# A graph layer on one core: x low by adding loads, counts relieved in pairs, zero products, and the order of two small steps

## What is computed

```python
HW = h @ W                                  # h = x, 1250 x 512; W 512 x 512
s, t = HW @ a[:512, 0], HW @ a[512:, 0]
e = leaky_relu(s[row] + t[col], 0.2)        # 21250 edges (row, col)
att = softmax of e over the edges of each row
agg = segment_sum(att[:, None] * h[col], row)
basis = b_splines(agg)                      # 8 cubic splines per element
out = silu(agg) @ base_w.T + einsum('nip,oip->no', basis, spline_w)
y = layernorm(x + out)                      # eps 1e-5
```

## Time and profile before

| what | us |
|---|---|
| median of 3 runs | 402.86 (401.79 to 402.97) |
| the profiled execution | 401.4 |
| its span, first to last instruction | 399.6 |
| busy in the span: PE, DVE, ACT | 383.4, 349.3, 264.0 |

### The profile page before, as it was taken

How to read it: one execution, slowest core, us unless ns; L and a number is a source line. 1 busy time by engine, 2 the same in 40 slices (tenths; PEclk the granted TensorE clock), 3 DMA queues, 4 the chain that set the end, 5 groups by cost and what they waited for, 6 DMA issues and landing times.

```text
span 399.6 us, 5094 instructions
## 1 busy us (share of the span) xinstructions
PE 383.4 (96%) x1888; PEld 297.2 (74%) x1888; DVE 349.3 (87%) x449; ACT 264.0 (66%) x273; POOL 33.3 (8%) x86
## 2 busy tenths in 40 slices
PE   5998879999999999999999999999999999999993
PEld 2556537788888888778888888887777777777782
DVE  8999988998677698999899999889999899979254
ACT  2669955574556879865786765868668786755213
POOL 4100110000000001001010101010010101010000
PEclk9999999999999999999999999999999999999999
DMA  7950491000000049546546464713332553723102
GB/s 260 334 152 2 59 266 45 2 0 0 2 0 2 0 133 317 157 120 187 169 120 191 116 179 133 211 53 105 107 99 58 158 168 96 248 62 106 54 26 99
DMA packets 23466, 45.90 MB, mean 115 GB/s; under 512 B 1846, under 2 KB 2058, under 8 KB 23442
## 3 DMA queue, kind: packets, MB, share of 16 engines
q0 software_dynamic: 11872, 23.01, 22.3%
q1 hardware_dynamic: 11570, 22.57, 17.1%
HBM read 43.02 MB, written 2.56 MB: 114 GB/s over the span
## 4 chain that ended last, share of the span: by engine, by line
PE 83%; DVE 11%; issue 2%; ACT 2%; DMA 1%; DVEq 0%; ACTq 0%
PE PS L1218 62%; PE PS L1159 15%; DVE oh L417 5%; DVE still L431 3%; PE PS L1139 2%; PE PS L1116 1%; PE PS L1169 1%; PE PS L1091 1%; ACT ex L881 1%; ACT ex L888 1%; DMA ei<-in_edges 1%; ACT ph L896 1%; PE PS L1071 0%; DVE scrap L654 0%; DVE ex L684 0%
## 5 line engine op out<-in xcount | busy, mean ns | idle before, releaser
L1218 PE MATMUL PS<-wh,s 128*128 128x512 f32 (+1 forms) x720 | 224.6, 392 | 0.1
L1218 PEld LDWEIGHTS PS<-wh,s 128*128 128x128 f32 (+1 forms) x720 | 133.4, 185 | 33.1 <-issue 1.5
L1218 PE MATMUL PS<-wl,s 128*128 128x512 f32 (+1 forms) x360 | 141.1, 392 | 0.0
L1218 PEld LDWEIGHTS PS<-wl,s 128*128 128x128 f32 (+1 forms) x360 | 66.8, 185 | 15.4
L947 ACT ACTIVATE s<-v 128x1280 fp32r<-128x1280 f32 (+1 forms) x32 | 40.0, 1250 | 44.1 <-DVE v L753 25.9
L930 ACT ACTIVATE v<-xt,bias 128x1280 f32<-128x1280 f32 (+1 forms) x32 | 42.9, 1339 | 18.9 <-DVE s L763 17.9
L747 DVE SCALAR_TENSOR_TENSOR v<-v,v 128x1280 f32<-128x1280 f32 (+1 forms) x32 | 46.5, 1453 | 5.1 <-ACT v L933 5.1
L753 DVE SCALAR_TENSOR_TENSOR v<-v,v 128x1280 f32<-128x1280 f32 (+1 forms) x32 | 46.7, 1461 | 3.3
L763 DVE SCALAR_TENSOR_TENSOR s<-v,s 128x1280 fp32r<-128x1280 f32 (+1 forms) x32 | 46.5, 1453 | 3.0 <-ACT s L947 3.0
L749 DVE SCALAR_TENSOR_TENSOR v<-v,v 128x1280 f32<-128x1280 f32 (+1 forms) x32 | 46.5, 1453 | 0.0
L408 POOL DMA_DIRECT2D wh<-in_splT x32 | 22.9, 716 | 275.3 <-PE PS L1218 186.3
(11 more groups left out here) (139 smaller groups left out, 354.8 us busy)
## 6 DMA issues: line engine op xcount, KB each, us to landing
wh<-in_splT POOLq DMA_DIRECT2D x32, 512.0 KB, 4.2
wring<-in_splT SPq DMA_DIRECT2D x21, 512.0 KB, 4.0
xt<-in_xT SPq DMA_DIRECT2D x1, 2500.0 KB, 11.3
xh<-in_x POOLq DMA_DIRECT2D x1, 2304.0 KB, 9.9
out<-xr SPq DMA_DIRECT2D x9, 256.0 KB
wh<-in_baseT POOLq DMA_DIRECT2D x4, 512.0 KB, 5.6
xl<-in_x POOLq DMA_DIRECT2D x1, 1536.0 KB, 12.5
wring<-in_baseT SPq DMA_DIRECT2D x3, 512.0 KB, 4.4
```

What stands on the lines that cost most here:

```text
L1218: m = e.matmul(PS[0:rows(w), w % 8, :], sx[:, ic, tl * 128:tl * 128 + rows(w)], wx[:, ic, :], start=first and n == 0, stop=last and n == 2)
```

## The change

All ten blocks of x low are now made by negation and adding loads: ACT negates block k in batch 8 + k, POOL's queue adds blocks 0 to 5 after the sixth negation and blocks 6 to 9 by two more loads after the tenth; xn, its loads and `x_low` are gone. xl and xt trade places in the memory, and x high is loaded once WT and a have landed. The counts of stretches 0 to 21 are relieved in pairs, 22 to 24 one by one. In batches 14 to 19 PE adds two products with zeros to the open bank. `greatest(3)` moves ahead of `p_low(1)`. EPS becomes the bias of the square root, and the scaling of the last five blocks stands right behind their own moments.

```diff
-        NEGATIVE_AT = {11 + k: k for k in range(ADDED)}
+        NEGATIVE_AT = {8 + k: k for k in range(NT)}
+        TAKEN = [(w, 2) for w in range(0, 22, 2)] + [(22, 1), (23, 1), (24, 1)]
+        WARM_AT = range(14, NB - 1)
...
-            e.dma_start(xn[:, ADDED:NT - 1, :], x[128 * ADDED:1152, :].rearrange("(w p) i -> p w i", p=128)
-                        ).then_inc(s_xn, 16)
-            e.dma_start(xn[0:LASTP, NT - 1, :], x[1152:N, :]).then_inc(s_xn, 16)
...
-            e.wait_ge(s_xt, 16)
+            e.wait_ge(s_w, 32)
             e.dma_start(xh[:, 0:NT - 1, :], x[0:1152, :].rearrange("(w p) i -> p w i", p=128)).then_inc(s_xh, 16)
             e.dma_start(xh[0:LASTP, NT - 1, :], x[1152:N, :]).then_inc(s_xh, 16)
...
             e.wait_ge(s_neg, ADDED)
             e.dma_start(xl[:, 0:ADDED, :], x[0:128 * ADDED, :].rearrange("(w p) i -> p w i", p=128), accum_op=ALU.add
                         ).then_inc(s_xa, 16)
+            e.wait_ge(s_neg, NT)
+            e.dma_start(xl[:, ADDED:NT - 1, :], x[128 * ADDED:1152, :].rearrange("(w p) i -> p w i", p=128),
+                        accum_op=ALU.add).then_inc(s_xa, 16)
+            e.dma_start(xl[0:LASTP, NT - 1, :], x[1152:N, :], accum_op=ALU.add).then_inc(s_xa, 16)
...
-            for k in range(ADDED, NT):
-                x_low(k)
...
             small(2)
+            greatest(3)
             p_low(1)
             inverse(0)
             inverse(1)
             weigh(2)
             inverse(2)
-            greatest(3)
             small(3)
...
                 e.bn_aggr(mv[0:p, k, :], st[0:p, k, :]).then_inc(s_bna, 1)
-                e.wait_ge(s_bna, w + 1)
-                e.tensor_scalar(sd[0:p, k:k + 1], mv[0:p, k, 1:2], EPS, None, ALU.add).then_inc(s_var, 1)
...
                 moments(w)
-                if w > 5:
-                    scale(w - 1)
-            scale(NT - 1)
+                scale(w)
...
-            def evacuate_counts(w):
-                ps = PS[:, w % 6, 0:CW].rearrange("p (b a) -> p a b", a=NT)
-                d = slice(DW * w, DW * w + DW)
-                e.wait_ge(s_ct, LAST_TILE[w] + 1)
-                e.copy(C[:, :, d], ps).then_inc(s_cnt, 1)
+            def evacuate_counts(w, n):
+                ps = PS[:, w % 6:w % 6 + n, 0:CW].rearrange("p w (b a) -> p a w b", a=NT)
+                c, z = (t[:, :, DW * w:DW * (w + n)].rearrange("p a (w b) -> p a w b", w=n) for t in (C, Z))
+                e.wait_ge(s_ct, LAST_TILE[w + n - 1] + 1)
+                e.copy(c, ps).then_inc(s_cnt, 1)
...
-                e.wait_ge(s_var, w1)
-                e.activation(a, a, ACT.Sqrt).then_inc(s_root, 1)
+                e.wait_ge(s_bna, w1)
+                e.activation(sd[0:p, k], mv[0:p, k, 1], ACT.Sqrt, bias=eps[0:p, :]).then_inc(s_root, 1)
...
+            def keep_warm(n, bank=6, start=True):
+                for k in range(n):
+                    e.matmul(PS[:, bank, 0:CW], nought[:, 0:128], nought[:, :], start=start, stop=start)
...
+                if b in WARM_AT:
+                    keep_warm(2, w % 6, start=False)
...
                 if j == 0 and i == 2:
-                    e.wait_ge(s_xlo, NT - ADDED)
-                    e.wait_ge(s_xa, 16)
+                    e.wait_ge(s_xa, 48)
```

More of the change, by code:

```diff
@@ L72 @@
 SETUP = {n: k + 1 for k, n in enumerate(
-    ["im", "mid", "tile", "nought", "id0", "ident", "xpad", "bigb", "wpad", "half", "down", "up"]
+    ["im", "mid", "tile", "nought", "id0", "ident", "xpad", "bigb", "wpad", "half", "eps", "down", "up"]
     + [f"bias{p}" for p in range(2 * NP + 1)] + ["lplace", "turn", "limits"])}
@@ L175, in build @@
         l_at = [R + 10 * W4 + 2048, R + 11 * W4 + 2048] + [R + k * W4 for k in range(2, 8)] + [
-            k * W4 for k in range(5)] + [19 * SLOT, 19 * SLOT + W4]
+            k * W4 for k in range(5)] + [15 * SLOT, 15 * SLOT + W4]
         wl = [at(f"wl{k}", 0, [128, 2, F], F32R, o) for k, o in enumerate(l_at)]
-        xr = at("xr", 21, [128, 5, F])
-        s_edge, s_dn, s_w, s_xt, s_xn, s_xh, s_xa, s_xr, s_out = (sem(f"s_{n}") for n in (
-            "edge", "dn", "w", "xt", "xn", "xh", "xa", "xr", "out"))
+        xr = at("xr", 17, [128, 5, F])
+        s_edge, s_dn, s_w, s_xt, s_xh, s_xa, s_xr, s_out = (sem(f"s_{n}") for n in (
+            "edge", "dn", "w", "xt", "xh", "xa", "xr", "out"))
         s_wr = [sem(f"s_wr{i}") for i in range(NWR)]
@@ L187, in build @@
         s_setup = sem("s_setup")
[L189 to L190 removed]
+        (s_reach, s_bits, s_col, s_mk, s_bound, s_left, s_tab, s_mv, s_head, s_ovk, s_ovm, s_ovs, s_ova, s_ovz, s_tmax, s_small, s_top, s_p, s_den, s_rden, s_plo,
+         s_a3, s_b3, s_spl, s_slo, s_wlo, s_res, s_bns, s_bna, s_rstd, s_nb, s_fin) = (
             sem(f"v_{n}") for n in (
[L192 to L193 removed]
+                "reach", "bits", "col", "mk", "bound", "left", "tab", "mv", "head", "ovk", "ovm", "ovs", "ova", "ovz", "tmax", "small", "top", "p", "den", "rden", "plo",
+                "a3", "b3", "spl", "slo", "wlo", "res", "bns", "bna", "rstd", "nb", "fin"))
         (s_lk, s_sq, s_neg, s_war, s_wa, s_srow, s_trow, s_scol, s_cnt, s_hole, s_e1, s_e2, s_phi, s_ya, s_ev, s_abs, s_q2, s_a2,
@@ L225, in done, with taken @@
             return min(TB * b + TB, NV)
+        def taken(w):
+            return next(k + 1 for k, (v, n) in enumerate(TAKEN) if v <= w < v + n)
         def within(v, lo, hi):
@@ L368, in _ @@
             e.memset(half[:, :], 0.5).then_inc(s_setup, 1)
+            e.memset(eps[:, :], EPS).then_inc(s_setup, 1)
             e.iota(way[:, 0, :], [[-1, 2]], base=NC, channel_multiplier=-2,
@@ L832, in st_rows @@
                     e.copy(strow[32 * k:32 * k + 2, 0:hi - lo], PS[32 * k:32 * k + 2, 6, 0:hi - lo]).then_inc(s_srow, 1)
-            def evacuate_counts(w):
-                ps = PS[:, w % 6, 0:CW].rearrange("p (b a) -> p a b", a=NT)
-                d = slice(DW * w, DW * w + DW)
-                e.wait_ge(s_ct, LAST_TILE[w] + 1)
-                e.copy(C[:, :, d], ps).then_inc(s_cnt, 1)
+            def evacuate_counts(w, n):
[3 more added lines that the diff above has]
+                e.copy(c, ps).then_inc(s_cnt, 1)
                 if w == 0:
                     e.wait_ge(s_setup, SETUP["bigb"])
-                e.activation(Z[:, :, d], ps, ACT.Relu, bias=bias[:, 2 * NP + 1:2 * NP + 2], scale=-BIG).then_inc(s_hole, 1)
+                e.activation(z, ps, ACT.Relu, bias=bias[:, 2 * NP + 1:2 * NP + 2], scale=-BIG).then_inc(s_hole, 1)
             for b in range(NB):
-                for w in range(ND):
-                    if LAST_TILE[w] // TB == b:
-                        evacuate_counts(w)
+                for w, n in TAKEN:
+                    if LAST_TILE[w + n - 1] // TB == b:
+                        evacuate_counts(w, n)
                 if b == WA_AT[-1]:
@@ L860, in _ @@
                     k = NEGATIVE_AT[b]
+                    r = rows(k)
                     e.wait_ge(s_xh, 32)
-                    e.wait_ge(s_sr, 1)
-                    e.mul(xl[:, k, :], xh[:, k, :].bitcast(F32), -1.0).then_inc(s_neg, 1)
+                    e.mul(xl[0:r, k, :], xh[0:r, k, :].bitcast(F32), -1.0).then_inc(s_neg, 1)
                 if b == SC_AT:
@@ L949, in roots @@
             def roots(w0, w1):
-                p = rows(w1 - 1)
-                a = sd[0:p, w0 % 5:w0 % 5 + w1 - w0]
-                e.wait_ge(s_var, w1)
-                e.activation(a, a, ACT.Sqrt).then_inc(s_root, 1)
+                p, k = rows(w1 - 1), slice(w0 % 5, w0 % 5 + w1 - w0)
+                e.wait_ge(s_bna, w1)
+                e.activation(sd[0:p, k], mv[0:p, k, 1], ACT.Sqrt, bias=eps[0:p, :]).then_inc(s_root, 1)
             def scale(w):
@@ L1004, in _ @@
                 if u == HU + 7:
+                    e.wait_ge(s_setup, SETUP["eps"])
                     roots(0, 5)
@@ L1111, in _ @@
                     left = loaded(e, r_size, 4, 5, 1, LND * NC)[0]
-            def keep_warm(n):
-                for k in range(n):
-                    e.matmul(PS[:, 6, 0:CW], nought[:, 0:128], nought[:, :], start=True, stop=True)
             e.wait_ge(s_scol, 3)
```

24 lines of the change are left out of this document (7 added, 17 removed).

## The result

| what | before | after |
|---|---|---|
| median, us | 402.54 (401.79 to 402.97) | 399.87 (399.79 to 400.28) |
| the profiled execution, us | 401.4 | 399.86 |
| its span, us | 399.6 | 398.1 |

The ratio is 0.9933 [0.9914, 0.9952]: faster by 0.5 to 0.9%, where 402.4 and no difference had been forecast. Between the two profiled executions lie 1.54 us, between the medians 2.67. So there are two questions: where the 1.54 come from, and why before's median lies 1.1 above its profiled execution while after's lies on it.

The account below looks back on a forecast made before the run. PE was taken as the bound, with 83% of the chain at full clock. +1.26 - 1.16 - 0.54 = -0.44 us, from 402.86 (profiled 401.4 plus 1.46) to 402.4; its own range 401.5 to 403.2, overall 400.9 to 403.7.

Parts of the forecast that it names:

- the zero products, +1.26: Batches 17 to 19 of the counts: six products of 0.21 us on PE's path, +1.26 us, bounds 0 to 2.5.
- I carry that along: Whole kernel: the 1.46 us by which the median lies above the profiled execution, added to the forecast unchanged.
- Rival A: Counting stage: zero products cost nothing, 401.2 us, or hold PE's clock in timed runs, 401.0 us; chance 27%.
- no cost: POOL's queue: weight loads behind the adding loads are first read after the last sums, so nothing is lost.
- `greatest(3)`: First sums: block 3's greatest t ahead of p_low(1) lets block 2's sum start sooner, -1.16 us (0.91 to 1.48).
- x low by adding loads: First sums: loads land near 51 and 52 to 59, use at 61.5, so zero on the path.
- B: First product with x low: adding loads land late, PE stands 2 to 2.5 us, 404.4 to 404.9 us; chance 8%.
- the loads of xn and `x_low` are worth nothing: Ahead of the correction at 50.85: removing them and four DVE subtractions gains nothing, since DVE waits for PE.
- The pairs: Counts on ACT: relief two stretches at a time saves 0 to 3.3 us, offsetting 2.1 of negations; zero on path.
- Last scalings: Tail: root bias -0.07 and block 8's store issued sooner, together -0.54 us, bounds -0.3 to -0.9.
- the case named for the upper bound: Tail: -0.9 us if the last store, now alone in its queue, also lands sooner.
- C: First sums: reordering gives nothing, or pairs on ACT delay the last counts, +0.7, 403.6 us; chance 8%.

Follow-up runs that it names:

- after_skip17: Kernel after with negations earlier (two to a batch at first), no zero products in batch 17, two of 16 columns in batch 18: 399.73 us, ratio 0.9921.
- after_nowarm: Kernel after without the zero products in batches 14 to 19: 400.44 us, ratio 0.9952.
- before_warm: Kernel before plus the zero products in batches 14 to 19 alone: 402.19 us, ratio 0.9989.
- after_shift: Kernel after plus 46 products of 16 columns in batches 0 to 11: 401.16 us, ratio 0.9960.
- before_xl: Kernel before with all of x low by adding loads and the earlier load of x high, nothing else: 403.19 us, ratio 1.0020.
- after_best_xr: Kernel after with negations two to a batch at first, five zero products in place of eight ahead of the left-over product, xr loaded late: 401.38 us, ratio 0.9951.
- before_again: Kernel before, unchanged, measured once more: 402.72 us, ratio 1.0003.
- after_nopairs: Kernel after with all stretches of counts relieved one by one: 400.16 us, ratio 0.9933.
- after_tiny: Kernel after with its twelve zero products in batches 14 to 19 cut from 500 to 16 columns: 400.50 us, ratio 0.9941.

## Why the prediction was wrong

**Where it failed first: the zero products, +1.26.** The step put the six products of batches 17 to 19 on the path at full length "since the row's own products of this shape lie in the chain at full length". They do, and the last count ended 1.28 later. But the same chain held 0.70 us between the last count and the 8 products of L1116, which the prediction gave as two times, 48.01 and 48.71, and didn't ask about. Something other than PE's products ends that wait. In ten traces, in which the last count ends at 48.0 to 48.5, the wait is 0.59 to 1.01; in after_skip17 (48.9) it is 0.33, and in the six in which PE is further behind (49.3 in the kernel after) there is none. A delay of PE is paid by the wait first. On PE's queue stand there the waits for the table of left-over products, for the column of s and for trow, and the read of the number of left-over products. In the kernel before the last instructions that the first and the third wait for are these, on DVE and on ACT:

```profile
41.95 0.33 DVE L551 TENSOR_SCALAR r_rest<-r_rest,limit 1x169 int32<-1x169 int32 x1
...
46.37 0.37 ACT L874 COPY trow<-PS 128x256 f32<-128x256 f32 x1
```

Both are over by 46.74, and the column of s by 37.62, long before 48.01. That leaves the read, which the profile doesn't show by itself. Of +1.26 there came +0.50 in the kernel after, 0.25 of it the products' own (after_nowarm), and +0.47 in before_warm. The prediction's lower bound of 0 was for gaps "that the chain doesn't show"; this one it did show.

**Where it failed next: "I carry that along".** The sum was made against the profiled execution, 401.4, and the 1.46 to the median was added unchanged. It didn't stay. After's median lies on its profiled execution (399.87 and 399.86), and of the 2.67 us between the medians 1.13 come from there. Of the 1.46 itself, 0.32 were the median of three executions, which a fourth brought from 402.86 to 402.54, and about 0.3 the early start of the profiled one. Rival A had this, as an alternative to the price of the products, with 27% and 401.0. Both are true at once in before_warm, the one run in which nothing else changes: they cost half a microsecond and take away the long executions. In the kernel after they aren't all of it: after_nowarm keeps 2.1 of the 2.67, and after_shift, with all of them, has executions from 400.01 to 402.70. Two traces caught a fall of the clock, to 0.50 at 47 to 50 in before_xl and 0.53 at 54 to 56 in after_best_xr, behind a wait of PE of 0.46 and of 2 us. The rule that the prediction draws on (the Trainium skill, TensorE: Matmul & The Clock Gate, section on HAM oscillation) says that PE falls back to the lower clock when it idles too long between groups of products; that fillers then pay is the prediction's own conclusion. The second trace agrees with the rule, but the 0.10 us of work in the same 2 us of after_nowarm was followed by no fall. And the clock is not all: all of before's executions between 402.8 and 403.7 have a mean granted clock of 0.995 to 0.999, as the shorter ones have. The second thing found is the late landing of wh of unit 2, worth up to 0.95 at 165, which the prediction had left out with the words "no cost" for the weight loads. How the 1.1 divides between the clock, the landing and the later start isn't settled, since no trace of the kernel before fell on a long execution; both that there are have no stall at 165.

**What held.** `greatest(3)`: -1.16 forecast, -1.19 measured, with PE held by its transposes at 76.64, 0.36 ahead of the sum where 0.35 was taken. x low by adding loads: zero at the first sums; the forecast issues of 38.5 and 44.5 were 38.9 and 44.9, the last landing 56.4 within 52 to 59, and B didn't come. That the loads of xn and `x_low` are worth nothing holds for the place where the prediction looked, the correction; at the start of the counts the traces without them are 0.45 sooner than five of the six with them (before_again). The pairs: zero, by after_nopairs. Last scalings: -0.54 forecast, -0.70 measured, within its bounds of -0.3 and -0.9; the part of the root was right (0.09 more on ACT where 0.12 was taken), and about 0.10 of the 0.16 more lies behind the issue of the last store, the case named for the upper bound. C, the reordering worth nothing, fell.

With +0.50 in place of +1.26 the same sum gives 0.50 - 1.16 - 0.54 = -1.20 and 401.7 us, inside the range. The rest, to 399.87, which is below the range, is above all what was carried along: it came out 0.0 above the profiled execution in place of 1.46. That this term was wrong is shown; what made it vanish is shown only in part.

## What to carry to other kernels

Ahead of work put on the critical engine, look for a wait with no releaser just behind it: that wait is cover and comes off the price. When the median lies a fraction of a per cent above the profiled execution, take a second profile of the same kernel to see whether the first is typical, ask which part of the change could act on the difference, and give it a term of the sum; it needn't stay. Filler products are judged by the spread of the executions as much as by the profile of one, and taking a few of them away again (5 for 8) may cost more than they do, which no run here shows by itself.

## What was not expected of the hardware

The granted clock fell to 0.50 in single executions only: the profiles of the kernel before show 1.00 throughout the same stretch in which that of before_xl has 3 us at 1.2 GHz. None of the 28 executions of before_warm, after, after_nopairs and after_skip17 has a mean granted clock under 0.995; after_shift, with all the zero products too, has two of eight at 0.992.

A weight load of 512 KB issued at the same point of the program landed after 5.2 to 9.3 us. What decides is neither the 1280 KB of xr beside it (8.9 without them), nor the place of the fetch alone (8.2 in after_tiny), nor PE's work alone (8.9 in after_shift); the same program gave the same landing each time it was seen (8.4 and 8.3 for before, 8.9 and 9.0 for after_nowarm).
